# K's head copies from two DMA queues in place of one (attention and feed-forward layers, one core)

## What is computed

```python
qp = (layernorm(x) @ w_q + b_q)            # 112 x 256 per batch
kp, vp = split(ctx @ w_kv + b_kv)          # 375 x 256 each, per batch
attn = softmax(einsum('bhqd,bhkd->bhqk', qp, kp) * SCALE)
x = x + einsum('bhqk,bhkd->bhqd', attn, vp) @ w_out + b_out
```

## Time and profile before

| | us |
|---|---|
| median of 3 runs | 1206.97 (1189.10 to 1209.06) |
| profiled execution, its own time | 1208.91 |
| its span, first to last instruction | 1207.1 |
| granted TensorE clock, mean | 0.786 of full |

### The profile page before, as it was taken

One profiled execution on the slowest core, in us unless ns is written; L12 is line 12 of the kernel. 1 busy time (PEld: TensorE's weight loads), 2 busy tenths in 40 slices (PEclk: granted clock), 3 DMA queues, 4 the chain that ended last, 5 costly groups with the idle time before them and its releaser, 6 DMA issues. The chain is left out here.

```text
span 1207.1 us, 16389 instructions
## 1 busy us (share of the span) xinstructions
PE 877.7 (73%) x6423; PEld 741.1 (61%) x6423; DVE 592.1 (49%) x1333; ACT 318.2 (26%) x422; POOL 82.2 (7%) x32
## 2 busy tenths in 40 slices
PE   0666788769176899999999993676888889923213
PEld 0555666557145799999999993555667666721003
DVE  6543444443534645354454535654444334257975
ACT  1322233333210424233332310322222222202410
POOL 0100000000200221313122100000000000000000
PEclk9976766885575999999999997679887776555556
DMA  3222222220400021111201002122221111020001
GB/s 107 40 63 52 52 52 39 40 40 1 150 0 1 35 70 36 62 43 35 69 35 35 1 1 79 24 59 60 55 55 41 31 30 24 1 71 1 1 0 30
DMA packets 44190, 48.93 MB, mean 41 GB/s; under 512 B 9920, under 2 KB 41824, under 8 KB 44128
## 3 DMA queue, kind: packets, MB, share of 16 engines
q1 hardware_dynamic: 44128, 48.07, 15.8%
HBM read 28.65 MB, written 0.92 MB: 24 GB/s over the span
## 5 line engine op out<-in xcount | busy, mean ns | idle before, releaser
L58 PE MATMUL ex_y<-w_parts,h_parts 128*112 128x256 f32 x1536 | 184.6, 281 | 0.0
L58 PEld LDWEIGHTS ex_y<-w_parts,h_parts 128*112 128x112 f32 x1536 | 183.9, 175 | 0.6
L58 PE MATMUL ex_h<-xnt,w_parts 128*128 128x448 f32 x768 | 161.9, 370 | 3.9 <-ACT h_full L1101 3.9
L58 PEld LDWEIGHTS ex_h<-xnt,w_parts 128*128 128x128 f32 x768 | 145.5, 191 | 16.4 <-ACT h_full L1101 5.1
L398 ACT ACTIVATE a_e<-a_pair 125x896 f32<-125x896 f32 x96 | 88.1, 918 | 199.2 <-PE a_pair L751 197.6
L1101 ACT ACTIVATE h_full<-ex_h,b_e 128x448 f32<-128x448 f32 x128 | 81.2, 636 | 213.5 <-PE ex_h L58 208.5
L723 PE MATMUL a_s<-a_kst,a_qst 48*112 48x376 f32 x256 | 62.8, 487 | 69.2 <-DMA a_kst<-a_kp 43.9
L1059 POOL TENSOR_TENSOR w_parts<-w_stage,w_parts 128x2048 fp32r<-128x2048 f32 x16 | 73.3, 4583 | 550.7 <-ACT w_parts L1071 550.7
L519 DVE CUSTOM_DVE_ANT_0 a_masked<-a_s,a_mask 112x375 f32<-112x375 f32 x128 | 65.3, 543 | 91.0 <-issue 90.9
L1234 DVE SCALAR_TENSOR_TENSOR x_sb<-ex_y,comb,x_sb 112x256 f32<-112x256 f32 x64 | 30.9, 484 | 134.0 <-PE ex_y L58 134.0
L515 DVE TENSOR_REDUCE a_mx<-a_s 112x2 f32<-112x750 f32 x64 | 59.9, 937 | 67.3 <-PE a_s L723 67.0
(11 more groups left out here) (260 smaller groups left out, 923.2 us busy)
## 6 DMA issues: line engine op xcount, KB each, us to landing
a_kst<-a_kp SPq DMA_DIRECT2D x384, 47.0 KB, 2.1
w_stage<-in_L_ffn_W SPq DMA_DIRECT2D x16, 1024.0 KB, 5.3
a_ctx<-in_ctx SPq DMA_DIRECT2D x16, 375.0 KB
wu<-in_L_ffn_w SPq DMA_DIRECT2D x1, 1024.0 KB
wd<-in_L_ffn_w SPq DMA_DIRECT2D x1, 1024.0 KB
x_sb<-in_x SPq DMA_DIRECT2D x1, 896.0 KB
out_x<-x_sb SPq DMA_DIRECT2D x1, 896.0 KB
a_w_raw<-in_L_xattn_w_kv SPq DMA_DIRECT2D x2, 256.0 KB, 2.9
```

Of the source, the lines that this page charges most:

```text
L58: ins = nc.tensor.matmul(out, a, b, start=first and k == 0 and n == 0, stop=last and k == len(w) - 1 and n == 2)
```

## The change

The 24 copies of a batch are shared out. `spread_k` becomes a function of the issuing engine, of e and of the slots. SP issues those with e = 0 (first heads): 8 of the high part, then, after its wait for the low part, 4. ACT issues those with e = 1: 8 in `spread_upper`, 4 in `spread_lower`, with the same waits. In the loop `spread_upper(b + 2)` stands on ACT between the exponential of (1,0) and values(b + 2, 0), and `spread_lower(b + 2)` between output(b - 1) and the exponential of (1,1). Ahead of the loop they stand around the two values of batch 0. The semaphores and their counts stay.

```diff
+                def spread_k(eng, b, e, slots):
+                    for slot in slots:
+                        part = int(slot == 1)
+                        for n in range(4):
+                            src = 32 * n + 16 * e
+                            dst = 64 * e + DH * slot
+                            eng.dma_start(kst[dst:dst + DH, b % 3, n:HP:4].bitcast(F32),
+                                          kp[src:src + DH, part].bitcast(F32)).then_inc(kst_in[b % 3], 16)
...
-                        def spread_k(b):
+                        sp.wait_ge(filled, n_fill)
+                        for b in range(B):
                             if b >= 3:
                                 wait_filled(sp, "s2", b - 3, 1, 2)
                             sp.wait_ge(k_hi, n_khi * (b + 1))
-                            for slot, part in ((0, 0), (2, 0), (1, 1)):
-                                if part:
-                                    wait_read(sp, "k", b)
-                                for n in range(4):
-                                    for e in range(2):
...
+                            spread_k(sp, b, 0, (0, 2))
+                            wait_read(sp, "k", b)
+                            spread_k(sp, b, 0, (1,))
                             if b + 3 < B:
                                 wait_filled(sp, "ct", b)
                                 load_ctx(b + 3)
...
+                        def spread_upper(b):
+                            if b >= 3:
+                                wait_filled(act, "s2", b - 3, 1, 2)
+                            act.wait_ge(k_hi, n_khi * (b + 1))
+                            spread_k(act, b, 1, (0, 2))
+
+                        def spread_lower(b):
+                            wait_read(act, "k", b)
+                            spread_k(act, b, 1, (1,))
...
                         keys(0)
+                        spread_upper(0)
                         values(0, 0)
                         values(0, 1)
+                        spread_lower(0)
...
                                 exps(b, 1, 0)
                             if b + 2 < B:
+                                spread_upper(b + 2)
                                 values(b + 2, 0)
                             if b >= 1:
                                 output(b - 1)
+                            if b + 2 < B:
+                                spread_lower(b + 2)
                             if 0 <= b < B:
                                 exps(b, 1, 1)
                                 exps(b, 1, 2)
```

## The result

The changed kernel took 1259.6 us (median of four runs, 1251.0 to 1279.7), the kernel before 1206.6 beside it: a ratio of 1.049, interval 1.025 to 1.074. Run once more next to the experiments it took 1260.7 against 1197.4, 1.040 (1.030 to 1.049). It is slower by four to five per cent. I had forecast +1.2%. The time lies inside the range of 1185 to 1275, but outside the forecast's own 1208 to 1236, and outside the band of 2% around no change to which I had given the best chance (0.48).

A forecast was written before the change was run, and what follows sets the result against it. TensorE's 15 waits for K copies, limited by SP's issue time, were taken as the bound; 58.1 us of added ACT delays less 43.9 removed gave +14.2, so 1223.1 us (+1.2%), range 1185 to 1275.

The forecast's parts named there:

- The copy waits: TensorE's 15 waits for copies of K before the score products of L723, in both layers: all gone, -43.9 us.
- ACT's price: Each copy issued by ACT costs 0.656 us as on SP: 5.25 us for eight, 2.6 for four.
- The places of the delay: Where TensorE next needs ACT, in passes of both layers and ahead of the loops: delays summing to 58.1 us.
- the query products: Ahead of each loop, behind ACT's 12 issues and its weight and x activations: +6.65 us, layer 1 +6.6, together 13.3.
- the first full pass: First full pass of each layer, no output between eight and four issues: scores +5.3 us, layer 1 +4.4, together 9.7.
- the sign that I had named: TensorE would wait for the exponential at L398 before L751 (layer 0) and L745 (layer 1), which it never did before.
- The clock: TensorE's granted clock, falling from 1.00 to 0.50 in the old wait: nothing put in the sum for any shift.
- clock lost: Rival: clock also falls at the new mid-pass stall, 2.2 us in 12 passes, 27 us, 1250 us; chance 0.13.
- clock regained: Rival: the old fall of TensorE's clock goes with the old copy wait, 27 us back, 1196 us; chance 0.07.
- Cheap issue: Rival: ACT issues a copy in 0.39 us, the eight behind the exponential of (1,0) deciding; 1181 us; chance 0.12.
- Activation first: Rival: ACT finishes its running activation before it issues, 15.6 us more in all, 1239 us; chance 0.14.
- Taking turns: Rival: SP's and ACT's issues hold each other up, 6.5 us more in 16 places, 105 us, 1328 us; chance 0.11.

The follow-up runs named there:

- work in the stalls: Changed kernel plus unread products on TensorE, 20 ahead of the output's transposes and 12 ahead of scores (1,2) in a pass; 1227.1 us, ratio 1.020.
- half on GpSimd: From the kernel before: second heads' copies of batches 1 to 7 issued by GpSimd with their own semaphores, batch 0 all on SP; 1125.7 us, ratio 0.932.
- work in the old copy wait: Kernel before plus 12 unread 128x64 products on TensorE ahead of the wait for the copies, passes b = 0 to 6; 1239.0 us, ratio 1.020.
- relief alone: Changed kernel with ACT's copies left out: SP issues 12 per batch, second heads' rows of K stay zero, result not right; 1123.0 us, ratio 0.934.
- ACT at the end of the pass: Changed kernel, but ACT issues only 4 copies per batch, behind values (b + 2, 1); SP the other 20 and all of batch 0; 1144.5 us, ratio 0.949.

## Why the prediction was right or wrong

**The copy waits: right.** All 15 gone, 43.9 us.

**ACT's price: right.** I took 0.656 us with the gaps; eight issues took 5.36 us (0.67) and four 2.59 (0.65), between the prices at which the sum would have been zero (0.566) and +2% (0.72).

**The places of the delay: right.** Scores (1,2) came 3.4 us later in a pass of layer 0 (+3.2 forecast), the query products 7.4 us (+6.65), the first full pass waited 5.2 us (+5.3). The added waits sum to 52.5 us where I had 58.1, the net to 11.2 where I had 14.2. Much of it showed one step earlier than the sign that I had named, as a wait of the transposes for the values (L799, +19.0) and not of the scores for the exponential.

**The clock: wrong, the term that was mis-sized.** The sentence was "As idle time moves and hardly shrinks, I put nothing in the sum." The profile shows +21.5 us, and that of the execution of 1279.7 us +56.5. The medians show a loss of 53 and 63 us where waits explain 11. That the total still fell inside the range is no merit of the sum: the range was wide for the sake of the rivals. The experiment with work in the stalls shows the cause. The rival "clock lost" priced it at 2.2 us in 12 passes, 27 us; measured are 2.5 us a pass in layer 0 and 3.0 in layer 1, 27.4 in the ten steady passes. Its place was right, its price was that of the fastest execution and half that of the slowest, and its total, 1250, is the nearest to what was measured. I gave it 0.13.

The reason for putting nothing down was that a clock term of either sign seemed to cancel. The two stalls aren't alike. The old one stands where the clock falls in layer 0 in any case: without it (half on GpSimd) busy time there is 112.4 us where it was 111.4, so removing it gave no clock back. The new one stands in a stretch that ran at 1.00 in two passes of layer 0 and in layer 1, so it took clock away there. In layer 1 the clock was lower with either stall, and the gain of having neither is 25.7 us in five passes. But work in the old copy wait did not keep the clock up, in layer 1 either, so for that wait it isn't shown that idleness is what brings the clock down. The rival "clock regained" (27 us back) was right in kind where the wait is taken away: relief alone gained 31 us by the medians beyond its copy waits, half on GpSimd 44 (47 and 45 of busy time in the profiles). It did not come true while the stall was only moved.

The Trainium skill, page TensorE: Matmul & The Clock Gate, section HAM oscillation — how this bites in real kernels, describes a kernel in which a wait in every tile drops the clock for the start of the next, each time. Layer 1 agrees in part, by the rows above: 0.80 with the copy waits, 0.71 with the stalls behind ACT and 1.00 with neither, for the same work, though work put into the copy wait did not help. I had not weighed that section.

**The other rivals fell.** Cheap issue: 615 ns. Activation first: ACT's first issue is at 229.97, in the exponential that runs from 229.86 to 230.78. Taking turns: with both queues at work the medians are 594 and 615 ns, and SP alone had 593. The Trainium skill has a rule of one generator locked for each in turn (page Perfetto Trace Analysis, section Per-instruction lifecycle). No run here shows a wait of that kind: whatever part of an issue is under the lock is too short to be seen in the medians.

**The divided pages.** The Trainium skill's advice to balance the copies over the engines that can issue them (page Perfetto Trace Analysis, section DMA Optimizations) holds for GpSimd (0.932) and for ACT at the end of the pass (0.949), and not for ACT with twelve copies in the place of this change (1.040).

**What would show it.** I had named a clock differing by over 0.05 as a sign of error. By the five passes it is 0.72 to 0.66 and 0.80 to 0.71. That was the right thing to look at, and it deserved more than 0.13.

## What to carry to other kernels

Moving DMA issues to another engine moves their time into that engine's program: put them on an engine that is idle in that stretch (GpSimd here), or behind the last operation of the pass on which the bound engine depends. Price a new stall on TensorE with the clock as well as its length, by asking whether the stretch behind it runs at full clock today; a stall moved from where the clock is low anyway to where it is high costs more than it returned. For a doubt of that kind, fill the stall with unread products that aren't longer than it: where the time falls, as for the stalls behind ACT, idleness was what cost the clock. Where it doesn't, as for the old copy wait, the doubt stays. And compare more than one profile of a kernel before a difference in busy time is read as an effect.

## What the runs showed of the hardware

- ACT issues a copy of this shape within SBUF in 615 ns at the median and SP in 593; SP is not slowed when ACT issues beside it (594). ACT's issue starts while its activation ahead still runs (229.97, in the one from 229.86 to 230.78).
- GpSimd issues it in 504 ns, and the copies of that kernel, SP's and GpSimd's together, landed after 2.5 us at the median in place of 2.1. I had not expected GpSimd to be the cheapest.

```profile
L316 POOL DMA_DIRECT2D a_kst<-a_kp x168: 504/504/644, 68.7 to 931.3; - x168
...
DMA to landing us min/median/max: 2.0/2.5/3.5
```

- The clock was worth about as much as the waits: the same 6423 products took 830 to 934 us over these profiles, by where TensorE stood still and, for one and the same kernel, 899 or 934 by the execution.
- The clock can fall from 1.00 to 0.50 while TensorE is busy without a break (212 to 216 us in the run with twelve products). What brings it down there stays open.
